# Attention scores: block-diagonal matmuls over the whole TensorE, or one head per matmul on strips of 32 rows

## The chip, the cores and the metric

The program runs on one core of one Trainium2 chip. What counts is the device time of one execution in microseconds. All engines start together; the time is that of the last instruction. The numbers on single instructions come from one profiled execution.

## What is computed

The reference is one transformer layer over 16 sequences of 128 tokens with 128 features. Cross attention with 16 heads of 8 dimensions each is followed by a mixture of experts with the two best of eight experts for each token.

```python
Q = _split_heads(q @ Wq.T)      # q is the layernorm of x
K = _split_heads(k @ Wk.T)      # k, v are the context
V = _split_heads(v @ Wv.T)
scores = jnp.einsum('bhqd,bhkd->bhqk', Q, K) / scale
scores = jnp.where(mask, NEG_INF, scores)
attn = jax.nn.softmax(scores, axis=-1)
out = jnp.einsum('bhqk,bhkd->bhqd', attn, V)
...
x = x + _L0_xattn_ref(_layernorm(x, axis=-1), ctx_1024, ctx_1024, mask_BxS2_if1, ...)
x = x + _L0_ffn_ref(_layernorm(x, axis=-1), L0_ffn_wg, L0_ffn_w1, L0_ffn_w3, L0_ffn_w2)
```

The scores of one head are a product over 8 features only. The kernel keeps float32 accuracy by splitting each value into a high and a low part of the float32r type.

## The kernel before, in words

Each engine runs a list of instructions written out by hand, and semaphores join the lists. The attention takes the 16 sequences (batches, `b` or `n`) in four quartets `u` of `QB = 4`. A fifth turn of the outer loop, `u == NQ`, finishes the last quartet.

**Stacks.** `front(u)` projects a quartet: for each group `g` of four heads it makes a query stack and a key stack in `st[:, u % 2, is_k, g, :]` with matmuls of 512 columns (L528). A stack has four strips of 32 partitions (`R = 32`), one for each head `j` of the group. In a strip lie the 8 features three times (as high, low and high parts in matching order) and two rows (24 and 25) that carry the mask. Rows 26 to 31 are not used.

**Scores twice.** The kernel forms every score tile twice. The first time queries are on the partitions (bank `s1`, L693), and VectorE takes the maximum over the keys of each (L1411). The second time keys are on the partitions (bank `s2`, L679), and ScalarE takes the exponential (L923) into `prob`. Before that the maximum must be subtracted: `m_neg` is rounded, transposed on TensorE (`transpose_maxima`), copied to `mT` (L1334), spread by GpSimd to a block form `m_bd` (L1026, four operations of 128x512 for a quartet), and added by a matmul with `ones_b` (L676) into the same bank.

**Block diagonals.** One matmul with 128 rows does the four heads of a group at once. Its moving operand has 512 columns, in which head `j` is nonzero only in strip `j` and in its own 128 columns. These operands are the slots `bd_slot(k, n)`; ScalarE clears six of them once (`clear_diagonal`, L810), and SyncE's queue copies the strips of the stacks into them, four DMAs of 64 KB for each slot (`block_diagonal`, L427; two of the first slot's by GpSimd's queue, L1018). TensorE waits for them in `diagonal_in`.

**Order of the work.** In the turn `u`, step `b`, group `g`, TensorE does the scores with keys on the partitions of quartet `u - 1` (batch `b`), then those with queries on the partitions of quartet `u` (batch `b - 1`). So step 0 of a turn has the former alone, steps 1 to 3 have both, and step 4 the latter alone. Between them come `values(n)` (L652, 16 products of 32 output rows on four column strips, each product two instructions), two transposes of the heads (L545), one back (L551) and the output projection (L558). Turn 0 has only the products for the maxima, turn 4 only those for the exponentials, together with routing and the preparation of the expert weights. The last 100 us are the experts.

`s1` has a ring of two banks (four in turn 0), `s2` a ring of two. TensorE waits for `max_done` and `prob_ready` before it reuses them. DVE waits for `s1_full`, ScalarE for `s2_full`.

## Time and profile before

| what | value |
|---|---|
| device time, median of 3 runs | 288.39 us (286.16 to 289.48) |
| span of the profiled execution | 289.2 us |
| TensorE busy, matmul | 220.1 us (76%) |
| VectorE (DVE) busy | 214.5 us (74%) |
| ScalarE (ACT) busy | 131.9 us (46%) |
| GpSimd (POOL) busy | 109.8 us (38%) |
| mean granted TensorE clock | 0.877 |

The profiled execution has no time of its own besides its span. The span is 0.8 us above the median and within the three runs. Busy time is summed over the whole span; which engine sets the time differs from stretch to stretch. A matmul's recorded duration includes its passage through the array, so the rate at which matmuls follow each other is read from the distance between their starts.

### The profile page before, as it was taken

The page shows a single profiled execution, that of the slowest core. Times are in us where ns is not written, and L with a number is a line of the kernel's source. Part 1 is how long each engine was busy: PE and PEld are TensorE (multiplying, and loading weights), DVE is VectorE, ACT ScalarE, POOL GpSimd, SP SyncE. Part 2 cuts the span into 40 slices and gives each one's busy share as a digit, 9 for nine tenths or more (in the row PEclk, how much of TensorE's full clock was granted, in tenths as well). Part 3 has the DMA queues.
Part 4 walks back from the last instruction along what each step waited for, and adds up shares of the span by engine and source line. Part 5 has one row for each costly group of instructions (what it writes and reads, how often), then busy time and mean ns, then how long its engine had stood idle before and what let it go on. Part 6 is the DMA issues. An engine that isn't in the chain of part 4 may idle for free.

```text
span 289.2 us, 5289 instructions
## 1 busy us (share of the span) xinstructions
PE 220.1 (76%) x1445; PEld 161.4 (56%) x1445; DVE 214.5 (74%) x619; ACT 131.9 (46%) x291; POOL 109.8 (38%) x120
## 2 busy tenths in 40 slices
PE   0787779998989988887667674688787789997620
PEld 0663456666757665665336542477566668886410
DVE  4779966688759867895977786568895568775596
ACT  5777127554665448342145546243334435453300
POOL 4310350121403070105486556104556565555530
PEclk9996579999999999979756799589899999999855
DMA  6954411353033302331602110421342232211807
GB/s 216 318 233 118 131 35 28 92 125 86 9 98 96 94 0 67 87 100 47 207 9 67 46 39 29 99 47 30 77 79 76 82 84 73 80 52 26 236 5 217
DMA packets 38108, 26.33 MB, mean 91 GB/s; under 512 B 4748, under 2 KB 35726, under 8 KB 37696
## 3 DMA queue, kind: packets, MB, share of 16 engines
q1 hardware_dynamic: 34848, 19.76, 25.5%
q0 software_dynamic: 2656, 5.40, 6.1%
q10 hardware_dynamic: 576, 0.83, 0.9%
q8 instruction: 13, 0.21, 0.3%
q14 instruction: 15, 0.12, 0.2%
HBM read 12.32 MB, written 6.31 MB: 64 GB/s over the span
## 4 chain that ended last, share of the span: by engine, by line
PE 42%; DVE 30%; issue 10%; SPq 8%; DMA 4%; ACT 2%; POOL 1%; another core or an unknown queue 1%; DVEq 0%; ACTq 0%; POOLq 0%
SPq L427 8%; PE bank L528 8%; DVE m_neg L1411 6%; PE bank L759 4%; PE bank L760 3%; PE bank L733 3%; PE bank L652 3%; DMA bd<-st 3%; PE bank L746 3%; PE bank L736 3%; PE bank L693 2%; PE bank L676 2%; PE bank L734 2%; PE bank L679 2%; PE bank L534 2%
## 5 line engine op out<-in xcount | busy, mean ns | idle before, releaser
L1411 DVE TENSOR_REDUCE m_neg<-bank 128x4 f32<-128x512 f32 x64 | 43.5, 684 | 15.4 <-PE bank L693 15.0
L1048 POOL DMA_INDIRECT ys<-big x39 | 38.1, 976 | 40.0 <-DVE big L1447 19.2
L923 ACT ACTIVATE big<-bank 128x512 f32<-128x512 f32 x64 | 37.4, 597 | 20.9 <-PE bank L679 20.0
L797 ACT ACTIVATE st<-bank 128x128 fp32r<-128x128 f32 (+1 forms) x78 | 22.6, 330 | 31.6 <-PE bank L746 16.1
L1004 POOL DMA_INDIRECT xg<-rows,rows_i x24 | 24.6, 1027 | 31.8 <-DVE rows_i L1218 11.6
L693 PE MATMUL bank<-bd,st 128*128 128x512 f32 x64 | 31.1, 509 | 4.7 <-DMA bd<-st 3.8
L676 PE MATMUL bank<-m_bd,ones_b 128*128 128x512 f32 x64 | 31.3, 489 | 2.1 <-ACT big L923 1.9
L759 PE MATMUL bank<-bd,st 128*128 x78 | 24.3, 332 | 9.8 <-DVE big L1447 6.2
L1355 DVE SCALAR_TENSOR_TENSOR st<-st_hi,cst,bank 128x512 fp32r<-128x512 f32 x32 | 23.3, 747 | 11.3 <-ACT st_hi L797 9.0
L1026 POOL TENSOR_TENSOR m_bd<-mT,cst 128x512 fp32r<-128x512 f32 x16 | 17.3, 1110 | 30.1 <-DVE mT L1334 30.0
L679 PE MATMUL bank<-bd,st 128*128 128x512 f32 x64 | 27.1, 423 | 0.0
L961 ACT ACTIVATE big<-bank 128x256 f32<-128x256 f32 x39 | 15.1, 387 | 24.2 <-PE bank L736 18.7
L1474 DVE TENSOR_TENSOR big<-big,bank 128x256 f32<-128x256 f32 x39 | 16.3, 418 | 12.7 <-ACT big L961 7.6
L733 PE MATMUL bank<-bd,st 128*128 x39 | 19.8, 509 | 5.5 <-DVE st L1435 4.8
L759 PEld LDWEIGHTS bank<-bd,st 128*128 128x128 f32 x78 | 15.6, 199 | 14.0 <-issue 13.1
L693 PEld LDWEIGHTS bank<-bd,st 128*128 128x128 f32 x64 | 14.2, 224 | 13.5 <-issue 6.7
L760 PE MATMUL bank<-bd,st 128*128 x78 | 21.5, 296 | 0.0
L1440 DVE TENSOR_TENSOR st<-bank,st 128x256 fp32r<-128x256 f32 x39 | 16.5, 422 | 5.5 <-ACT st L797 3.4
L988 POOL TENSOR_SCALAR ve<-mv 128x4 f32<-128x4 f32 x8 | 1.8, 230 | 46.7 <-DVE mv L1077 46.7
L1447 DVE TENSOR_REDUCE big<-bank 128x128 f32<-128x256 f32 x39 | 16.4, 421 | 4.1 <-PE bank L760 2.6
L652 PE MATMUL bank<-big 128*32 128x128 f32 x512 | 19.0, 294 | 0.0
L676 PEld LDWEIGHTS bank<-m_bd,ones_b 128*128 128x128 f32 x64 | 13.4, 209 | 9.0 <-issue 4.7
(174 smaller groups left out, 514.0 us busy)
## 6 DMA issues: line engine op xcount, KB each, us to landing
bd<-st SPq DMA_DIRECT2D x126, 64.0 KB, 2.0
big<-xg SPq DMA_DIRECT2D x39, 64.5 KB
raw<-in_L_ffn_w SPq DMA_DIRECT2D x2, 1024.0 KB, 9.3
raw<-ys SPq DMA_DIRECT2D x6, 256.0 KB
x_all<-in_x SPq DMA_DIRECT2D x4, 256.0 KB, 4.5
rows<-in_mask_BxS_if POOLq DMA_DIRECT2D x4, 256.0 KB, 5.2
ctx_all<-in_L_ffn_w SPq DMA_DIRECT2D x1, 1024.0 KB
ctx_all<-in_ctx SPq DMA_DIRECT2D x3, 256.0 KB, 5.2
```

The lines of the kernel that those rows point to most:

```text
L652: last = nc.tensor.matmul(ob[n % 2][R * j:R * (j + 1), half * P:(half + 1) * P], va[(n // QB) % 2][:, ((n % QB) * 4 + half * 2 + i) * NJ + ...
L676: nc.tensor.matmul(s2[k % 2][:, :], ones_b[:, b, :], m_bd[:, NJ * g:NJ * (g + 1), :].rearrange("p h q -> p (h q)"), start=True, stop=False)
L679: nc.tensor.matmul(s2[k % 2][:, :], st[:, (u - 1) % 2, 1, g, b * S:(b + 1) * S], bd_slot(0, n)[:, g, :, :].rearrange("p j q -> p (j q)"), ...
L693: nc.tensor.matmul(s1[k % s1_ring(u)][:, :], st[:, u % 2, 0, g, (b - 1) * S:b * S], bd_slot(1, n)[:, g, :, :].rearrange("p j q -> p (j q)" ...
L733: nc.tensor.matmul(both, t_lo[n % 2], first_high[:, :, bass.ds(col[n], I)], start=True, stop=False)
L759: nc.tensor.matmul(o, g_hi[n % GR][:, c * P:(c + 1) * P], w, start=(c == 0), stop=False)
L760: last = nc.tensor.matmul(o, g_lo[n % GR][:, c * P:(c + 1) * P], w, start=False, stop=(c == 1))
L923: nc.scalar.activation(prob[n % 2][:, NJ * g:NJ * (g + 1), :].rearrange("p h q -> p (h q)"), s2[k % 2][:, :], ACT.Exp, scale=SCALE).then_i ...
L1004: pool.indirect_dma_start(xg, bass.IndirectOffsetOnAxis(rows_i[:, n, k:k + 1], 0), sent_rows(n // QB)[:, n % QB, k, :], None, bounds_check ...
L1048: pool.indirect_dma_start(ys, bass.IndirectOffsetOnAxis(xt[n % XR][:, D:RW].bitcast(I32), 0), y_sb[n % YR], None, bounds_check=PAIRS - 1, ...
L1355: nc.vector.scalar_tensor_tensor(st[:, u % 2, is_k, g, :], st_hi[:, n % SH, :].bitcast(F32), cst[:, (C_CK if is_k else C_CQ):(C_CK if is_k ...
L1411: nc.vector.tensor_reduce(m_neg[:, H * (b - 1) + NJ * g:H * (b - 1) + NJ * (g + 1)], s1[k % s1_ring(u)][:, :].rearrange("p (j q) -> p j q" ...
```

## The change

The block diagonals, `m_bd`, `ones_b` and `bd` go. A score tile of 128x128 is now one matmul of its own: `scores(keys, queries, g)` multiplies 32 rows of a key stack by 32 rows of a query stack, at `tile_position=(R * g, 0)`. Step `g` now takes strip `g` of all four stacks, that is the heads `4 i + g`, where `i` is the number of the stack. The products with keys on the partitions use strip `g`, those with queries on the partitions strip `(g + 2) % 4`, in alternation. Both semaphore waits of a step (for `prob_ready` and for `max_done`) stand ahead of both products.

The rounded maxima, high and low, now go into rows 26 and 27 of the query strips. The key stacks hold ones in these rows, so the product itself adds the maxima. For each quartet eight DMAs copy 16 rows of `mT` each into one row of `st`: six on SyncE's queue and two on GpSimd's. Clearing of `va[1]` moves from DVE to GpSimd. The order of heads in `va`, `prob` and the rows of `Wo` follows.

```diff
-    c[:, C_CK] = np.where((r >= 8) & (r < 16), -1.0, 0.0)
+    c[:, C_CK] = np.where((r >= 8) & (r < 16), -1.0, np.where((r == MAX) | (r == MAX + 1), 1.0, 0.0))
...
+    c[:, C_ONE + 1] = (r == MAX) | (r == MAX + 1)
...
+        def maxima_in(engine, u):
+
+            for j in range(NJ):
+                engine.wait_ge(max_in[j], 32 * (u + 1))
+
+        def place_maxima(engine, u, j):
+
+            for a in range(2):
+                engine.dma_start(st[R * j + MAX + a:R * j + MAX + a + 1, u % 2, 0, :, :].rearrange("p g (b q) -> p (g b) q", q=S).bitcast(F32),
+                                 mT[R * j + 16 * a:R * j + 16 * (a + 1), :]).then_inc(max_in[j], 16)
...
-            for u in range(NQ + 1):
-                if u == NQ:
-                    sp.wait_ge(work_full, slot["V", NQ - 1] + 1)
-                    sp.wait_ge(ck_ready, NQ)
-                    sp.dma_start(raw[2], w2).then_inc(in_w2, 16)
...
+            for u in range(NQ):
+                taken(sp, ("MT", u))
+                for j in range(NJ - 1):
+                    place_maxima(sp, u, j)
+            sp.wait_ge(work_full, slot["V", NQ - 1] + 1)
+            sp.wait_ge(ck_ready, NQ)
+            sp.dma_start(raw[2], w2).then_inc(in_w2, 16)
...
+            def keys_wait(n, g):
+
+                k = NG * n + g
+                if n % QB == 0:
+                    pe.wait_ge(max_in[g], 32 * (n // QB + 1))
+                if k >= 2:
+                    pe.wait_ge(prob_ready, k - 1)
+
+            def queries_wait(n, g):
+
+                k, u = NG * n + g, n // QB
+                if n % QB == 0 and g == 0:
+                    stacks_in(pe, u, 0)
+                    stacks_in(pe, u, 1)
+                if k >= s1_ring(u):
+                    pe.wait_ge(max_done, k - s1_ring(u) + 1)
+
+            def scores(keys, queries, g):
+
+                if keys is not None:
+                    keys_wait(keys, g)
+                if queries is not None:
+                    queries_wait(queries, g)
+                for i in range(NG):
+                    if keys is not None:
+                        u, b = divmod(keys, QB)
+                        rows, tokens = slice(R * g, R * (g + 1)), slice(b * S, (b + 1) * S)
+                        by_key = nc.tensor.matmul(s2[g % 2][:, i * P:(i + 1) * P], st[rows, u % 2, 1, i, tokens], st[rows, u % 2, 0, i, tokens],
+                                                  start=True, stop=True, tile_position=(R * g, 0))
+                    if queries is not None:
+                        v, c = divmod(queries, QB)
+                        own, mine = query_rows(g), slice(c * S, (c + 1) * S)
+                        part = slice(R * own, R * (own + 1))
+                        by_query = nc.tensor.matmul(s1[(NG * queries + g) % s1_ring(v)][:, i * P:(i + 1) * P], st[part, v % 2, 0, i, mine],
+                                                    st[part, v % 2, 1, i, mine], start=True, stop=True, tile_position=(R * own, 0))
+                if keys is not None:
+                    by_key.then_inc(s2_full, 1)
+                if queries is not None:
+                    by_query.then_inc(s1_full, 1)
...
-                            nc.tensor.matmul(s2[k % 2][:, :], ones_b[:, b, :],
-                                             m_bd[:, NJ * g:NJ * (g + 1), :].rearrange("p h q -> p (h q)"),
-                                             start=True, stop=False)
-                            nc.tensor.matmul(s2[k % 2][:, :], st[:, (u - 1) % 2, 1, g, b * S:(b + 1) * S],
-                                             bd_slot(0, n)[:, g, :, :].rearrange("p j q -> p (j q)"),
-                                             start=False, stop=True).then_inc(s2_full, 1)
...
-                            nc.tensor.matmul(s1[k % s1_ring(u)][:, :], st[:, u % 2, 0, g, (b - 1) * S:b * S],
-                                             bd_slot(1, n)[:, g, :, :].rearrange("p j q -> p (j q)"),
-                                             start=True, stop=True).then_inc(s1_full, 1)
...
+                        scores(QB * (u - 1) + b if u >= 1 and b < QB else None, QB * u + b - 1 if u < NQ and b >= 1 else None, g)
...
-            clear_diagonal(0)
-            clear_diagonal(1)
+            act.wait_ge(in_c, 16)
...
-            for j in range(2, NJ):
-                rows = slice(R * j, R * (j + 1))
-                pool.dma_start(bd_slot(1, 0)[rows, :, j, :].bitcast(F32), st[rows, 0, 1, :, 0:S].bitcast(F32)).then_inc(first_half, 16)
+            own(nc.gpsimd.memset(va[1][:, :, :], 0.0))
...
                 if u:
-
                     taken(pool, ("MT", u - 1))
-                    if u >= 2:
-                        pool.wait_ge(s2_full, NG * QB * (u - 1))
-                    for g in range(NG):
-                        nc.gpsimd.tensor_tensor(m_bd[:, NJ * g:NJ * (g + 1), :], mT[:, :].unsqueeze(1).to_broadcast([P, NJ, P]),
-                                                cst[:, C_HEAD + NJ * g:C_HEAD + NJ * (g + 1)].unsqueeze(2).to_broadcast([P, NJ, P]),
-                                                ALU.mult).then_inc(mbd_ready, 1)
+                    place_maxima(pool, u - 1, NJ - 1)
```

TensorE before, in turn 1 around the values of the second batch. L676 and L679 are the scores by key, L693 the scores by query, L652 the values, L551 and L558 the transpose back and the projection:

```order
L676 MATMUL bank3<-m_bd,ones_b 128x512
L679 MATMUL bank3<-bd,st 128x512
L693 MATMUL bank1<-bd,st 128x512
L652 MATMUL bank5<-big 32x128 x16
L551 MATMUL bank4<-cst,on 128x128
L676 MATMUL bank2<-m_bd,ones_b 128x512
L679 MATMUL bank2<-bd,st 128x512
L693 MATMUL bank0<-bd,st 128x512
L558 MATMUL bank4<-wo_s,onT 128x128
```

TensorE after, in turn 1 around the values of the first batch. L659 is the score by key, L665 by query, L627 the values:

```order
L659 MATMUL bank3<-st 128x128
L665 MATMUL bank1<-st 128x128
L659 MATMUL bank3<-st 128x128
L665 MATMUL bank1<-st 128x128
L627 MATMUL bank4<-big 32x128 x16
L659 MATMUL bank2<-st 128x128
L665 MATMUL bank0<-st 128x128
L659 MATMUL bank2<-st 128x128
L665 MATMUL bank0<-st 128x128
```

Three matmuls of 512 columns have become eight of 128, in alternation between two strips; the places of the values, transposes and projections in the row stay.

SyncE's queue before, from the last loads of the input to the table that the experts need:

```order
L404 DMA ctx_all<-in_ctx 128x512
L414 DMA raw<-in_L_ffn_w 128x2048 x2
L427 DMA bd<-st 32x4x128 x122
L434 DMA ctx_all<-in_L_ffn_w 128x2048
L427 DMA bd<-st 32x4x128 x4
L460 TENSOR_LOAD tab
```

SyncE's queue after, the same piece:

```order
L400 DMA ctx_all<-in_ctx 128x512
L410 DMA raw<-in_L_ffn_w 128x2048 x2
L378 DMA st<-mT 1x16x128 x24
L418 DMA ctx_all<-in_L_ffn_w 128x2048
L434 TENSOR_LOAD tab
```

The load of the third expert weight now stands behind the maxima of the last quartet.

## Rows read from the trace of the kernel before

**Rows 1.** Page, the chain that ended last: share of the span by engine.

```profile
PE 42%; DVE 30%; issue 10%; SPq 8%; DMA 4%; ACT 2%; POOL 1%; another core or an unknown queue 1%; DVEq 0%; ACTq 0%; POOLq 0%
```

**Rows 2.** Windows: stretch, its length, busy time of each engine, clock, DMA share, GB/s.

```profile
25.59:38.77 13.18, 10.40 (x24) 5.69 (x25) 12.62 (x32) 3.08 (x5) 3.12 (x4) 0.57 0.43 115
...
51.66:69.47 17.81, 17.22 (x187) 11.79 (x188) 14.99 (x39) 9.73 (x21) 3.13 (x4) 1.00 0.44 105
...
113.86:145.12 31.26, 24.15 (x215) 17.24 (x216) 25.14 (x81) 9.98 (x23) 8.29 (x9) 0.85 0.39 108
145.12:188.48 43.36, 29.43 (x214) 19.18 (x215) 30.48 (x109) 20.87 (x44) 24.39 (x25) 0.74 0.18 50
```

**Rows 3.** Timeline of TensorE in turn 2: start, duration, line.

```profile
82.98 0.40 PE L693 MATMUL bank<-bd,st 128*128 128x512 f32 x1
83.31 1.08 PE L652 MATMUL bank<-big 128*32 128x128 f32 x32
84.32 0.50 PE L676 MATMUL bank<-m_bd,ones_b 128*128 128x512 f32 x1
84.66 0.39 PE L679 MATMUL bank<-bd,st 128*128 128x512 f32 x1
84.89 0.39 PE L693 MATMUL bank<-bd,st 128*128 128x512 f32 x1
85.12 0.40 PE L676 MATMUL bank<-m_bd,ones_b 128*128 128x512 f32 x1
```

**Rows 4.** Timelines of TensorE: narrower matmuls.

```profile
7.84 2.05 PE L600 MATMUL bank<-wvT,ctx_all 128*128 128x128 f32 x8 [7.84 <-DMA wvT<-in_L_xattn_Wv]
...
69.47 1.06 PE L600 MATMUL bank<-wvT,ctx_all 128*128 128x128 f32 x8
...
117.22 0.95 PE L572 MATMUL bank<-wgT,cT 128*128 128x8 f32 x8
...
239.43 0.28 PE L760 MATMUL bank<-bd,st 128*128 x1
239.55 0.28 PE L759 MATMUL bank<-bd,st 128*128 x1
```

**Rows 5.** Timeline of TensorE's weight loads, at the values of Rows 3.

```profile
83.31 0.81 PEld L652 LDWEIGHTS bank<-big 128*32 128x32 f32 x32 [0.37 <-issue]
```

**Rows 6.** Timeline of all engines where turn 0's scores begin.

```profile
18.78 3.57 DVE L1355 SCALAR_TENSOR_TENSOR st<-st_hi,cst,bank 128x512 fp32r<-128x512 f32 x5 [0.18 <-PE bank L528]
...
22.72 1.76 DVE L1123 MEMSET big<- 128x2048 f32 x1 [0.38 <-issue]
...
23.25 1.95 PE L693 MATMUL bank<-bd,st 128*128 128x512 f32 x4 [2.48 <-DMA bd<-st]
...
24.77 0.67 DVE L1411 TENSOR_REDUCE m_neg<-bank 128x4 f32<-128x512 f32 x1
```

**Rows 7.** Timeline of TensorE: first score by query of turn 3.

```profile
113.86 0.47 PE L693 MATMUL bank<-bd,st 128*128 128x512 f32 x1 [0.28 <-DMA bd<-st]
```

**Rows 8.** Page, costliest groups: busy us, mean ns, idle before and releaser.

```profile
L1411 DVE TENSOR_REDUCE m_neg<-bank 128x4 f32<-128x512 f32 x64 | 43.5, 684 | 15.4 <-PE bank L693 15.0
...
L923 ACT ACTIVATE big<-bank 128x512 f32<-128x512 f32 x64 | 37.4, 597 | 20.9 <-PE bank L679 20.0
```

**Rows 9.** The line of the block diagonals' DMAs: ns of issue, us to landing.

```profile
L427 SPq DMA_DIRECT2D bd<-st x126: 585/601/1538, 19.7 to 157.8; - x126
...
DMA to landing us min/median/max: 2.0/2.0/4.7
```

**Rows 10.** Timeline of all engines at the beginning of turn 4.

```profile
145.63 0.29 DVE L1334 COPY mT<-bank 128x128 f32<-128x128 f32 x1
...
147.43 0.76 PE L676 MATMUL bank<-m_bd,ones_b 128*128 128x512 f32 x1 [0.18 <-POOL m_bd L1026]
...
150.84 1.29 DVE L1314 TENSOR_TENSOR bd<-raw,bd 128x512 fp32r<-128x512 f32 x2
...
153.56 1.12 PE L534 MATMUL bank<-cst,st_hi 128*128 128x128 f32 x4 [2.96 <-DVE st_hi L1098]
```

157 lines of the change are left out of this document (41 added, 116 removed).

## The prediction

> **What bounds the kernel now.** I read the chain of work that ended last, then the windows, stage by stage, and then the timelines of single steps. The chain gives TensorE 42%, DVE 30%, and 12% to SyncE's queue and DMAs [rows 1]: three candidates, and the change touches all of them. The windows tell them apart [rows 2]. In turn 0 (25.59 to 38.77) DVE is busy 12.62 of 13.18 us, and TensorE's clock is mostly at its lower level: DVE bounds it. In steps 1 to 4 of turn 1 (51.66 to 69.47) TensorE is busy 17.22 of 17.81 us, DVE 14.99: TensorE bounds it, but DVE stands 2.8 us behind. Turn 2 repeats turn 1. In turns 3 and 4 (31.26 and 43.36 us) neither is above about 80%: there, chains from engine to engine set the pace. SyncE's queue is on the chain only because its DMAs run one behind the other, 0.60 us each to issue [rows 9]; what counts is where TensorE waits for them: 2.48 us once at the start [rows 6] and some 0.3 us at the first score by query of each of turns 1 to 3, of which turn 3's is shown [rows 7]. So the block diagonals' traffic and ScalarE's clearing weigh little, and the question is what TensorE's instructions cost.
>
> **The pair of scores on TensorE.** Before, a step has three matmuls of 512 columns, whose starts lie 0.23 us apart (84.66, 84.89, 85.12), so 0.70 us [rows 3]. After, it has eight of 128 columns, each with its own weights of 128 columns. No row shows a matmul on a strip of rows, nor a float32r matmul of 128 columns, so I bound both. A full-array matmul of only 8 columns costs at most 0.95/8 = 0.12 us, and one of 256 columns of float32r (the experts' L759, L760; `bd` is by then the expert weights) 0.12 us too [rows 4]: below 256 columns the load of 128 weight columns sets the rate. I estimate 0.112 for one. If the two strips in alternation work side by side, a step costs four of these, 0.45 us; if they take turns, eight, 0.90. For side by side speak the values: 32 instructions on four column strips take 1.08 us [rows 3] and their loads 0.81 [rows 5], a quarter of what 32 would take one after another. Those are column strips with narrow loads, so this is near, not the same. I take 0.45. One step saves 0.25 us, and the twelve steps with both products in a turn save 3.0.
>
> **What strips cost elsewhere.** The array must change between its whole, column strips and row strips. Into the values: the last L693 starts at 82.98 and would be through at 83.21; the values start at 83.31, 0.10 late. Out of them: eight waves of 0.11 from 83.31 end at 84.19; the next starts at 84.32, and its successor 0.34 later where 0.23 is usual, since its load was not hidden: 0.24 together [rows 3]. Before, a batch has two such changes. After, seven: the transposes L545, L551 and the projection L558 now also stand between row strips. Five more for each of four batches are 20 in a turn. Their load was partly exposed already, so I take the 0.10 for each, 2.0 us in a turn; at 0.24 it is 4.8. The Trainium skill ("TensorEngine Tiling (Array Packing)", Key Properties) says that changing the tiling mode drains TensorE. The gap at the values agrees with that; by it the changes cannot be free, and it speaks against this change. It also says that different tiles can load and multiply in parallel, which no trace here shows for strips of rows.
>
> The four steps 4 of turns 0 to 3 have only queries: 0.45 instead of 0.23 each group. DVE takes 684 ns for each maximum [rows 8] and hides that; without it, 0.9 us a turn. Turn 0 is the same at the lower clock: L600 there takes 2.05 us for eight instructions against 1.06 [rows 4], so a group costs up to 4 x 0.26 = 1.0, or less with the next strip beside it, against 13.18/16 = 0.82 of DVE: about even, up to 3 us if it is not.
>
> Both semaphore waits now stand ahead of the pair, so a score by key also waits for DVE's maximum two groups back; queued behind it are ScalarE's exponential and the values. In turns 1 and 2 DVE becomes the next bound: 14.99 of 17.81. That caps the gain at 2.8 a turn. **Turns 1 and 2: 2 x (-3.0 + 2.0) = -2.0 us**, between 2 x -2.8 and 2 x +1.8. **Turn 3**, where DVE and TensorE are both at some 80% [rows 2], half of that for one turn: **-0.5**, between -1.5 and +0.9.
>
> **The waits that go.** At the start the last stack is ready at 18.78 + 3.57 = 22.35, and the first matmul starts at 23.25; DVE meanwhile clears `va[1]` (22.72, 1.76 us) and takes its first maximum at 24.77 [rows 6]. After, both DMA and clearing are gone from here; four matmuls from 22.4 at up to 0.26 each let DVE start at about 23.3: **-1.5 us**, and all of it counts, since DVE bounds the turn. The memset on GpSimd lies in the idle time while TensorE makes the first stacks. The three waits of rows 7: **-0.9** (0 to -1.2); the wait for an exponential of the `s2` ring [rows 8] comes up behind them. ScalarE's six clearings, DVE's `ones_b` and GpSimd's `m_bd` run beside longer work: nothing.
>
> **The maxima by DMA.** From `mT` on, SyncE issues six DMAs of 0.60 us; each lands 2.0 us later [rows 9]. The first pair is in at +3.2 us, the third at +5.6; GpSimd's pair at about +3.4. In turns 1 to 3, the stacks of the next quartet (28 matmuls of 512 columns, 6.4 us at the distance of rows 3) stand between and hide it, if narrowly; were it not hidden, it would cost up to 5.6 a turn. In turn 4 nothing stands between: `mT` is ready at 145.92, so the first score comes at 149.1 instead of 147.43 and the third at 151.5 [rows 10]. Behind it are an exponential (0.6), two weight copies on ScalarE and then DVE's L1314, which began at 150.84 right behind other work; it begins about 0.5 us later. The fourth group waits for L534 at 153.56 anyway. **+0.5**, between 0 and +1.7. SyncE's load of the third weight moves behind the maxima, to about 149.5; its first user is tick 12 of 20 in a turn of 43 us. GpSimd loses four m_bd operations and gains two DMAs, so the row sends behind them come no later.
>
> **Turn 4 otherwise.** Sixteen groups of 0.45 instead of 0.47: nothing. Fifteen to twenty more changes of the array's form, some 0.10 each, half on the chain: **+0.9**, up to +3.
>
> **Sum:** -1.5 - 0.9 - 2.0 - 0.5 + 0.5 + 0.9 = -3.5 us. The span was 289.2 and becomes 285.7; set against the median of 288.4, that gives **284.9 us**. The experts' 100 us are untouched.
>
> **The rivals.**
> *A. Everything is hidden.* Changes of form cost nothing more, and DVE bounds turns 1 and 2: -5.6 there, -1.5 in turn 3, -1.5 - 1.2 at the waits, 0 in turn 4: -9.8, **278.6 us**. For it: DVE's 2.8 us; against it: the gaps in rows 3.
> *B. Changes of form cost 0.24 each.* +3.6 in turns 1 and 2, +0.9 in turn 3, +2.5 in turn 4, less 2.4: +4.6, **293 us**. Slower from about 0.16 for a change on.
> *C. Strips of rows take turns.* The change then doesn't do what its title says. A pair costs 0.90, 5.4 us more a turn than forecast, in turn 3 half: 13.5 above the forecast, **298 us**. Slower once a pair costs over some 0.57. Against it: rows 5.
> *D. A float32r matmul of 128 columns runs like plain float32.* L600, plain float32, needs two instructions for a product, up to 0.13 us each at the full clock, 0.26 at the lower [rows 4]. All float32r matmuls of before have 256 or 512 columns, so nothing in the trace excludes it. A pair then costs 0.7 to 1.0, turn 0 at the low clock up to 1.3 to 2 a group against 0.82: +8 there or more, +3.5 for turns 1 and 2 with the changes, +4 in turn 4, less 2.4: **about 301 us**.
>
> **How the numbers follow.** Forecast 0.42 (its own range 281 to 288), A 0.15, B 0.15, C 0.11, D 0.17. Three executions lay 3.3 us apart, so about 1% (2.9 us) is what a measurement can tell from no change. The forecast is faster by over 1% in three quarters of its range and A always: 0.47. Within 1%: a quarter of the forecast and a part of B and C: 0.19. Slower: 0.34. The range of 278 to 299 takes in A, the forecast, B and half of C and D.
>
> **What the profile after would show.** Starts of L659 about 0.11 apart with an L665 between, a pair of groups at 0.45 (right), 0.90 (C); two records for each product would be D. The first maximum near 23.3. Windows of steps 1 to 4 in turns 1 and 2 at about 16.8, DVE over 88% busy. The distance from the last L659 or L665 to a transpose and back prices a change of form. The first score of turn 4 about 3.4 us after `mT`. I would be wrong if DMAs into a single row took much longer than 2.0 us, or if DVE, waited for earlier now, held back the exponentials.

## The result, and the profile after

The changed kernel takes **318.28 us** (median of 4 runs, 317.71 to 321.57), the kernel before in the same runs 288.94 (286.16 to 291.12). The ratio is 1.109, with a 95% interval of 1.100 to 1.118. The prediction was 284.9, range 278 to 299: wrong in size and in sign. The span of the profiled execution is 315.9 us, 26.7 above the 289.2 of before. Executions of one kernel differ by their clock (e6 below: 300.5 us at a mean clock of 0.783, 316.9 at 0.718), so a median is of all of them, a ratio only of those within 1.5% of the fastest, and no ratio stands where the spread is wide.

The page of the kernel after, its busy time, its granted clock in 40 slices of the span (tenths, 9 is full), and the chain that ended last:

```profile
PE 251.4 (80%) x1765; PEld 204.6 (65%) x1765; DVE 213.4 (68%) x615; ACT 123.4 (39%) x285; POOL 96.3 (30%) x113
...
PEclk9996579555695555955555555555999999999755
...
PE 59%; DVE 21%; DMA 7%; issue 6%; ACT 4%; POOL 2%; SPq 0%; POOLq 0%; ACTq 0%; DVEq 0%
```

The same clock row of the kernel before:

```profile
PEclk9996579999999999979756799589899999999855
```

TensorE's share of the chain grows from 42% [rows 1] to 59%, and DVE's falls from 30% to 21%. The clock rows show why. Before, the clock is at its upper level (2.4 GHz) from turn 1's stacks through turn 2 and turn 3's stacks. After, it is at 5 tenths, the lower level (1.2 GHz), for most of turns 1 to 4. The mean granted clock is 0.709 against 0.877.

By stretch, the windows of the kernel after: turn 0; turns 1 and 2, each from its own last stack to the first stack of the next; turns 3 and 4; the experts. Columns as in rows 2; the clock is the third number from the right.

```profile
25.59:40.60 15.01, 12.31 (x73) 11.22 (x67) 13.44 (x33) 1.77 (x4) 3.10 (x4) 0.53 0.08 19
48.60:81.80 33.20, 30.25 (x287) 24.39 (x287) 19.00 (x48) 12.83 (x27) 3.10 (x4) 0.58 0.03 9
90.20:123.90 33.70, 30.35 (x287) 24.31 (x287) 19.95 (x56) 12.82 (x27) 2.54 (x3) 0.57 0.00 1
131.80:172.10 40.30, 35.60 (x307) 28.79 (x306) 28.43 (x90) 13.38 (x29) 9.35 (x10) 0.55 0.05 15
172.10:215.60 43.50, 34.52 (x237) 26.48 (x236) 27.07 (x102) 20.50 (x43) 18.82 (x21) 0.50 0.22 68
215.60:315.90 100.30, 71.25 (x445) 61.46 (x445) 73.95 (x232) 37.24 (x117) 46.82 (x48) 0.87 0.31 83
```

The same cuts of the kernel before (its turns 3 and 4 in one row):

```profile
47.70:70.60 22.90, 21.34 (x208) 14.22 (x206) 17.95 (x47) 13.01 (x28) 3.13 (x4) 1.00 0.42 101
78.30:102.30 24.00, 21.47 (x208) 14.30 (x206) 18.98 (x55) 13.64 (x29) 2.57 (x3) 1.00 0.35 88
109.90:185.00 75.10, 53.67 (x431) 35.43 (x429) 56.61 (x190) 33.45 (x72) 32.08 (x34) 0.81 0.26 71
185.00:289.10 104.10, 76.33 (x445) 63.83 (x445) 75.15 (x232) 36.61 (x118) 47.13 (x48) 0.88 0.33 85
```

Turn 1 loses 33.2 - 22.9 = 10.3 us, turn 2 loses 9.7, turns 3 and 4 together 83.8 - 75.1 = 8.7. The first stack matmul of turn 1 comes at 40.6 instead of 38.9, 1.7 late; the experts take 3.8 less, for which no cause was looked for. With +0.2 for the three blocks of stacks between, that is the 26.7. TensorE is above 90% busy in turns 1 and 2 and DVE at 57 to 59%: TensorE bounds them alone.

What happens inside turn 1, in finer windows of the kernel after:

```profile
48.60:51.40 2.80, 1.87 (x17) 1.53 (x16) 1.93 (x4) 2.48 (x6) 0.00 (x0) 1.00 0.00 0
51.40:53.70 2.30, 2.27 (x52) 2.00 (x52) 1.54 (x4) 1.56 (x3) 0.00 (x0) 1.00 0.00 0
53.70:60.00 6.30, 5.81 (x67) 4.61 (x67) 4.42 (x14) 2.56 (x5) 1.86 (x3) 0.50 0.01 4
...
81.80:84.40 2.60, 2.60 (x9) 1.94 (x8) 0.96 (x3) 1.34 (x3) 1.00 (x2) 0.50 0.03 7
84.40:90.20 5.80, 5.79 (x26) 4.29 (x24) 4.16 (x7) 4.09 (x7) 0.00 (x0) 1.00 0.05 11
```

The clock is still 1.00 in step 0 and the first pairs of step 1. At 53.7 it falls to 0.50, though TensorE is 92% busy from then on; it comes back at 84.4, in the stacks of turn 2, whose matmuls take 128 rows and 512 columns. The fall repeats in turns 2 and 3, just before 95 and 136; turn 4 has no stacks, and the clock stays at 0.50 from 136 to the end of turn 4. Being busy is plainly not what the clock goes by alone.

TensorE on both sides of that fall, in its timeline of the kernel after (L659 by key, L665 by query, L627 the values):

```profile
51.43 0.32 PE L659 MATMUL bank<-st 32*128 32x128 f32 x1 [0.20 <-ACT big L892]
51.44 0.32 PE L665 MATMUL bank<-st 32*128 32x128 f32 x1
51.60 0.27 PE L659 MATMUL bank<-st 32*128 32x128 f32 x1
51.60 0.27 PE L665 MATMUL bank<-st 32*128 32x128 f32 x1
...
51.92 0.32 PE L659 MATMUL bank<-st 32*128 32x128 f32 x1
...
52.31 0.27 PE L659 MATMUL bank<-st 32*128 32x128 f32 x1
...
52.51 1.08 PE L627 MATMUL bank<-big 128*32 128x128 f32 x32
...
57.34 0.41 PE L659 MATMUL bank<-st 32*128 32x128 f32 x1
...
57.55 0.41 PE L659 MATMUL bank<-st 32*128 32x128 f32 x1
...
58.10 1.93 PE L627 MATMUL bank<-big 128*32 128x128 f32 x32
```

The strips do what the title says. L659 and L665 start within 0.01 us of each other, and a pair of groups takes 51.92 - 51.43 = 0.49 us. From the last of a pair to the values are 0.20 us (52.31 to 52.51), where 0.11 is usual between products: the change of form costs 0.09. After the fall the same products stand 0.21 apart (57.34, 57.55) instead of 0.11, and the values take 1.93 us instead of 1.08.

### The profile page after: what moved, and what is told of

It reads as the page before. It is cut to its first block, busy times and chain, and to the rows that moved or that the text cites. A ratio compares the mean times of both kernels' runs of the same rounds, so it can differ in the third digit from the quotient of the medians.

```text
span 315.9 us, 5743 instructions
## 1 busy us (share of the span) xinstructions
PE 251.4 (80%) x1765; PEld 204.6 (65%) x1765; DVE 213.4 (68%) x615; ACT 123.4 (39%) x285; POOL 96.3 (30%) x113
## 4 chain that ended last, share of the span: by engine, by line
PE 59%; DVE 21%; DMA 7%; issue 6%; ACT 4%; POOL 2%; SPq 0%; POOLq 0%; ACTq 0%; DVEq 0%
PE bank L659 12%; PE bank L502 9%; PE bank L627 7%; DVE m_neg L1360 4%; PE bank L665 4%; PE bank L532 3%; PE bank L519 3%; PE bank L508 3%; PE bank L742 2%; PE bank L716 2%; DMA ys<-big 2%; PE bank L719 2%; PE bank L717 2%; PE bank L525 2%; PE bank L743 2%
## 5 line engine op out<-in xcount | busy, mean ns | idle before, releaser
L659 PE MATMUL bank<-st 32*128 32x128 f32 x256 | 51.5, 386 | 5.7 <-ACT big L892 2.9
L659 PEld LDWEIGHTS bank<-st 32*128 32x128 f32 x256 | 43.2, 282 | 16.2 <-issue 8.2
L665 PE MATMUL bank<-st 32*128 32x128 f32 x256 | 51.6, 404 | 2.6 <-DVE st L1305 1.9
L665 PEld LDWEIGHTS bank<-st 32*128 32x128 f32 x256 | 44.3, 298 | 5.7 <-issue 4.7
L1305 DVE SCALAR_TENSOR_TENSOR st<-st_hi,cst,bank 128x512 fp32r<-128x512 f32 x32 | 23.1, 748 | 12.1 <-ACT st_hi L864 12.1
L742 PE MATMUL bank<-weights,st 128*128 x78 | 23.0, 316 | 8.9 <-DVE big L1395 8.9
L627 PE MATMUL bank<-big 128*32 128x128 f32 x512 | 29.6, 407 | 0.0
L864 ACT ACTIVATE st_hi<-bank,cst 128x512 fp32r<-128x512 f32 x32 | 22.0, 688 | 12.9 <-PE bank L502 12.7
L716 PE MATMUL bank<-weights,st 128*128 x39 | 19.6, 501 | 7.1 <-DVE st L1383 7.0
L928 ACT ACTIVATE big<-bank 128x256 f32<-128x256 f32 x39 | 15.0, 384 | 22.9 <-PE bank L719 22.9
L627 PEld LDWEIGHTS bank<-big 128*32 128x32 f32 x512 | 21.2, 161 | 3.4 <-issue 0.3
L742 PEld LDWEIGHTS bank<-weights,st 128*128 128x128 f32 x78 | 14.9, 190 | 11.1 <-issue 9.8
L378 POOL DMA_DIRECT2D st<-mT x8 | 4.2, 529 | 58.1 <-DVE mT L1287 58.1
L743 PE MATMUL bank<-weights,st 128*128 x78 | 20.8, 286 | 0.0
## 6 DMA issues: line engine op xcount, KB each, us to landing
big<-xg SPq DMA_DIRECT2D x39, 64.5 KB, 1.9
```

The source lines that it names most:

```text
L627: last = nc.tensor.matmul(ob[n % 2][R * g:R * (g + 1), half * P:(half + 1) * P], va[(n // QB) % 2][:, (n % QB) * H + h, :], prob[n % 2][:, ...
L659: by_key = nc.tensor.matmul(s2[g % 2][:, i * P:(i + 1) * P], st[rows, u % 2, 1, i, tokens], st[rows, u % 2, 0, i, tokens], start=True, sto ...
L665: by_query = nc.tensor.matmul(s1[(NG * queries + g) % s1_ring(v)][:, i * P:(i + 1) * P], st[part, v % 2, 0, i, mine], st[part, v % 2, 1, i ...
L716: nc.tensor.matmul(both, t_lo[n % 2], first_high[:, :, bass.ds(col[n], I)], start=True, stop=False)
L742: nc.tensor.matmul(o, g_hi[n % GR][:, c * P:(c + 1) * P], w, start=(c == 0), stop=False)
L743: last = nc.tensor.matmul(o, g_lo[n % GR][:, c * P:(c + 1) * P], w, start=False, stop=(c == 1))
```

## The experiments

Fifteen more kernels ran. "Turn 1" is the same stretch as above, from the turn's last stack matmul to the next turn's first, with its granted clock.

| kernel | device time, median (lowest to highest), us | ratio to before, 95% | turn 1: us at clock | turn 2: us at clock |
|---|---|---|---|---|
| before | 288.94 (286.16 to 291.12) | 1 | 22.9 at 1.00 | 24.0 at 1.00 |
| after | 318.28 (317.71 to 321.57) | 1.109 (1.100 to 1.118) | 33.2 at 0.58 | 33.7 at 0.57 |
| e1_warm | 368.56 (357.57 to 375.70) | 1.244 (1.232 to 1.256) | 43.9 at 0.57 | 44.8 at 0.55 |
| e2_split | 302.41 (300.05 to 303.22) | 1.043 (1.036 to 1.051) | 27.3 at 1.00 | 28.3 at 1.00 |
| e3_wide | 357.57 (353.32 to 365.98) | 1.227 (1.217 to 1.237) | 35.4 at 0.82 | 45.6 at 0.57 |
| e4_dve_clear | 317.84 (313.72 to 322.82) | - | 29.2 at 0.71 | 34.7 at 0.54 |
| e5_full_rows | 306.37 (303.05 to 311.88) | - | 24.6 at 1.00 | 31.9 at 0.79 |
| e6_rows64 | 313.36 (300.50 to 316.87) | - | 31.6 at 0.63 | 35.1 at 0.54 |
| e7_q_strips | 302.78 (300.85 to 308.98) | 1.050 (1.041 to 1.059) | 28.0 at 1.00 | 29.1 at 1.00 |
| e8_k_strips | 338.46 (338.26 to 338.94) | 1.176 (1.169 to 1.183) | 40.0 at 0.57 | 41.3 at 0.59 |
| e9_k_strips_plus | 359.57 (347.44 to 363.29) | - | 45.5 at 0.59 | 46.8 at 0.60 |
| e10_q_strips_less | 329.16 (328.01 to 331.64) | 1.146 (1.139 to 1.153) | 36.4 at 0.62 | 39.5 at 0.56 |
| e11_max_rows | 308.47 (304.87 to 310.59) | 1.066 (1.060 to 1.073) | 30.8 at 0.78 | 31.4 at 0.89 |
| e12_k_strips_next | 330.47 (329.70 to 343.94) | 1.136 (1.126 to 1.145) | 41.5 at 0.63 | 33.3 at 0.90 |
| e13_max_rows_plus | 309.34 (308.42 to 310.86) | 1.065 (1.057 to 1.073) | 31.9 at 0.89 | 31.8 at 0.89 |
| e14_max_pool | 302.59 (301.34 to 309.78) | 1.050 (1.044 to 1.057) | 24.2 at 0.86 | 25.1 at 1.00 |
| e15_max_pool_plus | 304.76 (303.19 to 306.24) | 1.057 (1.051 to 1.064) | 24.4 at 1.00 | 25.0 at 1.00 |

The times of a turn come from one profiled execution of each kernel. It is the longest or nearly the longest of its kernel for e1 (375.7 us), e6 (316.5), e9 (363.3) and e11 (310.6), and the shortest or nearly so for e4 (313.7) and e5 (303.3); so the turns of different kernels compare only roughly.

### Does the fall of the clock depend on the rows that a product fills?

**e1_warm**: the changed kernel with one matmul of 128 rows and 512 columns ahead of every step's products.

```diff
+                if keys is not None or queries is not None:
+                    spot = s2[g % 2] if keys is not None else s1[(NG * queries + g) % s1_ring(queries // QB)]
+                    nc.tensor.matmul(spot[:, :], ws_hi[:, 0, 0, :], ws_hi[:, 0, :, :].rearrange("p g c -> p (g c)"), start=True, stop=True)
                 for i in range(NG):
```

> The changed kernel plus one matmul for each step, ahead of its products: all 128 rows, 512 columns, into the bank that the products then overwrite; its result is never used. 92 of them add 0.23 us each at the full clock, 21 us of work, and bring two more changes of the array's form a step. Theory 1 (the changed kernel is slow because TensorE's clock stands at its lower level through turns 1 to 4, and it does so because the scores now come as narrow matmuls on strips of rows): the clock in turns 1 and 2 comes back to 0.9 or more, and although work is added the time falls, to some 295 to 305 us. Theory 2 (the strips are slow by themselves, by changes of form and by the two waits ahead of a pair; the clock only follows an array that idles): the added work comes on top, 330 us or more.

Measured: 368.56 us. Turn 1 has TensorE busy for all of its 43.9 us, and the clock is at 0.57. One full product a step does not hold it up; this cure fails. The windows on both sides of the fall in turn 1:

```profile
60.30:69.50 9.20, 9.20 (x54) 6.72 (x52) 5.22 (x9) 6.76 (x11) 0.00 (x0) 1.00 0.00 1
69.80:107.60 37.80, 37.80 (x269) 28.11 (x269) 16.49 (x42) 9.61 (x20) 3.11 (x4) 0.50 0.03 8
```

TensorE has not paused once in the 9 us before the clock falls. So a wait just ahead is not needed for the fall; it came here without one.

**e2_split**: the kernel before, each of the products L679 and L693 cut in four of 128 columns; all keep 128 rows.

```diff
-                            nc.tensor.matmul(s1[k % s1_ring(u)][:, :], st[:, u % 2, 0, g, (b - 1) * S:b * S],
-                                             bd_slot(1, n)[:, g, :, :].rearrange("p j q -> p (j q)"), ...
+                            for j in range(NJ):
+                                last = nc.tensor.matmul(s1[k % s1_ring(u)][:, j * P:(j + 1) * P], st[:, u % 2, 0, g, (b - 1) * S:b * S],
+                                                        bd_slot(1, n)[:, g, j, :], start=True, stop=True)
```

> The kernel before with its L679 and L693 cut into four matmuls of 128 columns each, all 128 rows as before: 128 rows, narrow. Each takes 0.112 us instead of a quarter of 0.23, so a pair costs 0.23 + 8 x 0.112 = 1.13 us instead of 0.70. If the narrow matmuls, in which the load of the weights sets the rate, are what lets the clock fall, the clock in turns 1 and 2 falls to about 0.5 as in the changed kernel, and the time goes over 325 us. If it is the 32 rows, the clock stays at 1.0 in turns 1 and 2 and the time is that of the added 0.43 us a pair: 5 us in each of turns 1 and 2, some 3 in turn 3, a little in turns 0 and 4: 300 to 306 us.

Measured: 302.41 us, clock 1.00 in both turns. Narrow products alone cost 4.4 us in turn 1 (27.3 less 22.9) and leave the clock up.

**e3_wide**: the changed kernel, each product on its 32 rows but with 512 columns. The scores are then no longer the reference's, since each product runs over all four batches.

```diff
-                        by_key = nc.tensor.matmul(s2[g % 2][:, i * P:(i + 1) * P], st[rows, u % 2, 1, i, tokens], st[rows, u % 2, 0, i, tokens],
+                        by_key = nc.tensor.matmul(s2[g % 2][:, :], st[rows, u % 2, 1, i, tokens], st[rows, u % 2, 0, i, :],
```

> The changed kernel with each product on a strip 512 columns wide instead of 128: it multiplies a batch's keys by the queries of all four batches, over the whole bank, and so leaves out the right scores. 32 rows, wide. If 32 rows are what lets the clock fall, it stays at about 0.5 in turns 1 to 4, and a pair costs 4 x 0.43 = 1.7 us: 350 us or more. If narrow matmuls are, the clock stays at 1.0, a pair costs 4 x 0.23 = 0.92 and the time is 300 to 310 us, less than the changed kernel's 318 with four times the columns.

Measured: 357.57 us. The clock falls with wide products of 32 rows too. Turn 1 and turn 2 are the same program apart from a few small operations, 35.4 us at 0.82 and 45.6 at 0.57: a first price of the clock.

**e5_full_rows** and **e6_rows64**: the changed kernel with the same 128 columns, the same order and the same DMAs, on all 128 rows (e5), or on two strips of 64 (e6). Each product then sums over four or two heads, so the scores are not the reference's. Two more things change with it. The first group of a turn waits for all the maxima at once, and e5 has no changes of form between its products and the transposes and projections.

```diff
-                        by_key = nc.tensor.matmul(s2[g % 2][:, i * P:(i + 1) * P], st[rows, u % 2, 1, i, tokens], st[rows, u % 2, 0, i, tokens],
-                                                  start=True, stop=True, tile_position=(R * g, 0))
+                        by_key = nc.tensor.matmul(s2[g % 2][:, i * P:(i + 1) * P], st[:, u % 2, 1, i, tokens], st[:, u % 2, 0, i, tokens],
+                                                  start=True, stop=True)
```

> The changed kernel with every product of 128x128 on all 128 rows instead of 32: it adds up the scores of four heads, so the right scores are left out, and the same number of matmuls, the DMAs of the maxima and the joined waits remain. They can no longer run side by side: a pair costs 8 x 0.112 = 0.90 us at the full clock instead of 0.45. Theory 1 (32 rows let the clock fall, and the low clock is what costs): the clock in turns 1 and 2 stays at 1.0 and the time is 293 to 300 us, 20 below the changed kernel, though TensorE's products take twice as long side by side with nothing. Theory 2 (the structure of the change costs: number of matmuls, joined waits, maxima by DMA, changes of form): the time stays above 310 us.

> The changed kernel with 64 rows for each product, on two strips of 64: scores of two heads are added, the right ones left out. The two products of a pair stand on different halves in every step and can run side by side, 0.45 us a pair, with the same changes of form as in the changed kernel. It asks where between 32 and 128 rows the clock turns. If it stays at 1.0 in turns 1 and 2, the time is what I had forecast for the change itself, 283 to 290 us; if it falls as with 32 rows, 315 to 322.

Measured: e5 takes 306.37 us, 12 below the changed kernel, although its products no longer run side by side. In its timeline of TensorE they stand 0.11 us apart, a pair of groups 0.90, as the forecast had it for products in turn:

```profile
51.15 0.28 PE L665 MATMUL bank<-st 128*128 128x128 f32 x1
51.26 0.27 PE L659 MATMUL bank<-st 128*128 128x128 f32 x1
51.37 0.28 PE L665 MATMUL bank<-st 128*128 128x128 f32 x1
```

Its turn 1 keeps the clock and takes 24.6 us. The same order with 32 rows takes 33.2. So with half the speed for the scores the turn is 8.6 us shorter. The changes of form that e5 saves, put at 2.0 us a turn in the prediction, are less than the 5.4 us (12 x 0.45) that its products cost more; the clock makes the difference.

In turn 2 e5 loses a part of it, so 293 to 300 was too low:

```profile
84.00:97.40 13.40, 13.40 (x110) 12.29 (x109) 6.16 (x17) 3.86 (x7) 1.78 (x3) 0.50 0.01 2
97.80:112.40 14.60, 12.95 (x157) 11.83 (x155) 11.59 (x34) 7.01 (x16) 0.36 (x1) 1.00 0.00 1
```

The clock can fall without any strip, then, but it comes back inside the turn, while in the changed kernel it stays down until the next stacks. e6's executions run from 300.5 to 316.9 us, from below e5's fastest (303.1) to almost the changed kernel's; where between 32 and 128 rows the clock turns, it does not tell.

### What does a lower clock cost?

**e4_dve_clear**: the changed kernel, `va[1]` cleared on DVE behind turn 0's stacks, as before.

```diff
-            own(nc.gpsimd.memset(va[1][:, :, :], 0.0))
...
+                if u == 0:
+                    clear_values(1)
```

> The changed kernel with the clearing of va[1] put back from GpSimd to DVE, at the beginning of turn 0. In the changed kernel one of DVE's four normalisations waits for 2 us beside GpSimd's memset, and everything behind it starts 2 us later. If the memset is the cause, the first stack matmul starts 2.0 us earlier; DVE then spends 1.8 us on the clearing ahead of its first maximum, which partly stands beside TensorE's first products: a gain of 0 to 1.5 us, 317 to 318.5. If the pause has another cause, the stack starts as late as in the changed kernel and the time rises to 320.

Two things come out. First, the clearing on GpSimd was not free. The start of the kernel after, all engines:

```profile
8.20 4.07 DVE L1062 TENSOR_SCALAR rows<-x_all,mv,rstd 128x128 f32<-128x128 f32 x4 [0.47 <-POOL rstd L956]
...
10.06 1.81 POOL L981 MEMSET big<- 128x2048 f32 x1
...
14.01 0.77 PE L502 MATMUL bank<-ck_hi,ws_hi 128*128 128x512 f32 x1 [0.56 <-DVE ck_lo L1102]
```

and of e4:

```profile
8.21 2.07 DVE L1057 TENSOR_SCALAR rows<-x_all,mv,rstd 128x128 f32<-128x128 f32 x4 [0.48 <-POOL rstd L956]
...
12.01 0.76 PE L502 MATMUL bank<-ck_hi,ws_hi 128*128 128x512 f32 x1 [0.56 <-DVE ck_lo L1100]
```

With GpSimd's memset beside it DVE's four normalisations take 2.0 us longer, and TensorE's first stack comes 2.0 us later. Second, e4 has the program of the changed kernel from turn 1 on, yet its turn 1 takes 29.2 us at a clock of 0.71 instead of 33.2 at 0.58. In e4 the clock falls only at 60, two batches into the turn instead of one. So one stretch of the changed program can be seen at the upper level: from the values of the first batch to those of the second, in e4 and in the kernel before:

```profile
51.37:55.50 4.13, 3.49 (x69) 2.87 (x67) 3.72 (x13) 2.66 (x6) 0.45 (x2) 1.00 0.02 6
52.75:57.22 4.47, 4.47 (x48) 3.00 (x47) 3.55 (x13) 2.61 (x6) 0.51 (x2) 1.00 0.39 101
```

TensorE has 0.98 us less to do there, and the stretch is 0.34 us shorter: TensorE now waits, 0.64 us of it for a maximum of DVE, which is busy for 3.72 of 4.13 us. Four such stretches make a turn, for which the forecast was -1.0. The next one is 0.43 us longer than before (55.50 to 60.69 against 57.22 to 61.98), with its last 0.7 us at the lower clock, so one stretch does not stand for the turn.

The whole turn at full clock was not measured. An estimate: with 2 x (1 - 0.58) x 33.2 = 27.9 us at the lower level in turn 1 of the changed kernel and 16.9 in e4's, the 11.0 us between them cost 4.0, and without any the turn would take 23.1. If the 27.9 us all ran at half speed, it would be 19.3. My working for the turn, 22.9 - 1.0 = 21.9, lies between. The total is not clearly moved (317.84; 313.72 and 314.23 in two runs, 321.44 and 322.82 in two with a clock of 0.69).

### Which part of the change lets the clock fall?

**e7_q_strips**: the kernel before, only the scores by query on strips. **e8_k_strips**: the changed kernel, the scores by query back on block diagonals as one product of 512 columns; the clearing on DVE.

```diff
 e7
-                            nc.tensor.matmul(s1[k % s1_ring(u)][:, :], st[:, u % 2, 0, g, (b - 1) * S:b * S], ...
+                            for i in range(NG):
+                                last = nc.tensor.matmul(s1[k % s1_ring(u)][:, i * P:(i + 1) * P], st[part, u % 2, 0, i, mine],
+                                                        st[part, u % 2, 1, i, mine], start=True, stop=True, tile_position=(R * g, 0))
 e8
-                        by_query = nc.tensor.matmul(s1[...][:, i * P:(i + 1) * P], st[part, v % 2, 0, i, mine], ...
+                    nc.tensor.matmul(s1[(NG * queries + g) % s1_ring(v)][:, :], st[:, v % 2, 0, g, c * S:(c + 1) * S],
+                                     bd_slot(queries)[:, g, :, :].rearrange("p j q -> p (j q)"), start=True, stop=True).then_inc(s1_full, 1)
```

> One half of the change alone: the kernel before, with only the scores by query (L693) on strips of 32 rows; the scores by key stay as block diagonals with ones_b. A step is 2 x 0.23 us on the whole array, 4 x 0.11 on a strip and two changes of form at 0.2: 1.3 us at the full clock. Theory 1: the narrow strips again let the clock fall in turns 1 and 2, though over a third of the array's time is wide matmuls of 128 rows (the added fillers did not hold it either): 335 to 350 us. If wide matmuls in this share hold the clock: 305 to 315.

> The other half alone: the changed kernel with the scores by query back on block diagonals (16 slots of DMAs a kernel, three slots cleared, va[1] cleared by DVE), the scores by key on strips with the maxima in the spare rows. A step is 4 x 0.11 us on a strip, 0.23 on the whole array and two changes of form: 1.0 us at the full clock, against 0.70 before and 0.9 in the changed kernel at the low clock. Theory 1: low clock again, a step at 1.6 us or more: 330 to 345 us. If the clock holds: 300 to 308.

Measured: e7 302.78 us with a clock of 1.00 in turns 1 and 2, not the fall that theory 1 had, and a little below the 305 to 315 of the other case; e8 338.46 with 0.57 and 0.59. Strips of 32 rows do not bring the clock down by being there. A step of e7 has two full products and four on a strip, one of e8 one full product and four on a strip. The next three runs ask whether that is the difference.

**e10_q_strips_less**: e7 without L676, the matmul that adds the maxima.

```diff
-                            nc.tensor.matmul(s2[k % 2][:, :], ones_b[:, b, :],
-                                             m_bd[:, NJ * g:NJ * (g + 1), :].rearrange("p h q -> p (h q)"),
-                                             start=True, stop=False)
```

> The kernel e7 (before, with the scores by query as four matmuls of 32 rows) without the matmul that adds the maxima; it leaves that subtraction out, so its exponentials are not the reference's. A step now has one full product and four on a strip, as e8. By the count of work it should gain up to 16 x 0.23 = 3.7 us a turn: 290 to 298 us against e7's 302.8. Theory 1 (the share of full products decides the clock): the clock falls in turns 1 and 2 as in e8, their distance between stacks grows from 28 and 29 us to 35 to 42, and the whole takes 320 to 340 us, slower for less work. Rival (something else of e8 holds its clock down): the clock stays at 1.0 in turns 1 and 2 and the whole takes 290 to 300 us.

Measured: **329.16 us, 26 more for 64 matmuls less**. Turn 1 goes from 28.0 us at a clock of 1.00 to 36.4 at 0.62. In e7:

```profile
48.80:76.80 28.00, 26.89 (x255) 18.90 (x253) 18.53 (x47) 13.26 (x28) 3.11 (x4) 1.00 0.19 48
```

and in e10:

```profile
47.10:83.50 36.40, 35.28 (x239) 26.02 (x238) 19.16 (x48) 13.11 (x27) 3.10 (x4) 0.62 0.14 37
...
49.80:55.90 6.10, 6.09 (x58) 4.29 (x58) 3.62 (x11) 3.48 (x7) 0.00 (x0) 1.00 0.21 52
```

Here too TensorE is busy without a pause for the 6 us before the clock falls, at 56.

**e9_k_strips_plus** and **e12_k_strips_next**: the opposite, e8 with full products added. In e9 one stands ahead of the four strips in each of the 64 groups that have keys. In e12 it stands behind them, next to the other full product, and only where a group has both: 36 of them, 12 instead of 16 in each of turns 1 to 3 and none in turn 4.

```diff
 e9
+                if keys is not None:
+                    nc.tensor.matmul(s2[g % 2][:, :], ws_hi[:, 0, 0, :], ws_hi[:, 0, :, :].rearrange("p g c -> p (g c)"), start=True, stop=True)
                 for i in range(NG):
 e12
+                    if keys is not None:
+                        nc.tensor.matmul(s1[(NG * queries + g) % s1_ring(v)][:, :], ws_hi[:, 0, 0, :], ...
                     nc.tensor.matmul(s1[(NG * queries + g) % s1_ring(v)][:, :], st[:, v % 2, 0, g, c * S:(c + 1) * S],
```

> The kernel e8 (scores by query as one matmul of 512 columns on block diagonals, scores by key as four matmuls of 32 rows) with one more matmul of 512 columns and 128 rows ahead of each group's four products by key; its result is overwritten, so the output is e8's. At full clock these 64 matmuls cost 64 x 0.23 = 14.7 us. Theory 1, the granted clock depends on how much of TensorE's time goes to matmuls on the full array: the mixture of a step is now that of e7 (two full products and four on a strip), so the clock stays at 1.0 in turns 1 and 2, their distance between stacks falls from some 40 us to 28 to 30, and the whole takes 300 to 315 us, 20 us or more below e8's 338 although it does more. Rival, something else of e8 holds the clock down (the products by key on strips, the pairing under two waits, the DMAs into single rows): the clock stays low and the 64 matmuls are added at the lower rate, 345 to 365 us.

> The kernel e9, with the extra matmul of 512 columns and 128 rows directly ahead of the full score by query, so that the two full products of a step stand next to each other behind the four on a strip, as in e7. Its result is overwritten. Theory 2, the order decides (short pieces of full work between strips do not hold the clock, longer ones do): the clock stays at 1.0 in turns 1 and 2, the distances between stacks fall to 28 to 31 us, the whole takes 300 to 318 us. Rival, the clock falls for another reason of e8 (TensorE's waits in step 0 of a turn, and strips by key that carry the maxima): as e9, 347 to 363 us with a clock of 0.70 to 0.75.

Measured: e9 359.57 us, clock 0.59 and 0.60; the mixture of e7 is not enough, and the rival has it. e12 330.47 us, 29 less in the median and 18 between the shortest executions (347.4 and 329.7). It is not e9 in another order alone, as its expectation has it: it has 28 full products fewer, which at 0.23 us each (0.43 at the lower clock) are 6 to 12 us. Its turns are split; the windows of e12:

```profile
46.70:88.20 41.50, 39.09 (x251) 27.55 (x251) 18.48 (x47) 13.27 (x28) 3.10 (x4) 0.63 0.12 33
96.00:129.30 33.30, 29.16 (x251) 20.92 (x251) 19.56 (x55) 13.84 (x29) 2.55 (x3) 0.90 0.13 33
```

In steps 1 to 3 the two kernels have the same instructions in another order, so the order may play a part; but the missing products of step 0 changed with it, and the two were not separated. e12 did not hold the clock in turn 1, nor bring the time to the 300 to 318 expected. Two turns of nearly the same program have different clocks here: 41.5 us at 0.63, 33.3 at 0.90.

### The other half of the change alone

**e11_max_rows**: the kernel before with all its block diagonals; only the maxima go by DMA, straight into rows 26 and 27 of the query block diagonals, and L676, `m_bd` and `ones_b` go. It is the part of the change that takes work from TensorE without any strip.

```diff
-                            nc.tensor.matmul(s2[k % 2][:, :], ones_b[:, b, :], m_bd[...], start=True, stop=False)
...
+            for j in strips:
+                for a in range(2):
+                    row, at = R * j + MAX + a, R * j + 16 * a
+                    if b == 0:
+                        engine.dma_start(bd[row:row + 1, 3:6, :].rearrange("p k (g j q) -> p (k g) j q", g=NG, j=NJ)[:, :, j, :].bitcast(F32),
+                                         mT[at:at + 12, :]).then_inc(max_in[j // 2 * 2], 16)
+                    else:
+                        engine.dma_start(bd_slot(0, n)[row:row + 1, :, j, :].bitcast(F32), mT[at + 12:at + 16, :]).then_inc(max_in[1], 16)
```

> The other half of the change alone: before, with all products on block diagonals of 128 rows, but the maxima go by DMA into rows 26 and 27 of the query block diagonals (16 DMAs for a quartet, 12 on SyncE's queue and 4 on GpSimd's), and the matmul that adds them, its operand on GpSimd and the block of ones go. A step has two products of 512 columns in place of three. At full clock this takes 16 x 0.23 = 3.7 us out of TensorE in a turn, of which at most 2.8 count in turns 1 and 2 before DVE bounds them, half in turn 3; turn 4's first score comes up to 1.7 us later and DVE has some eight small operations more for each quartet. Theory 1 with the clock unharmed: -2.8 x 2 - 1.4 + 1 + 1 = -5, 283 us, between 279 and 287. Rival, the thinner mixture of full products lets the clock fall in turns 1 and 2: 292 to 305 us.

**e13_max_rows_plus**: e11 with a full product in the place of L676, its result overwritten.

```diff
+                            nc.tensor.matmul(s2[k % 2][:, :], ws_hi[:, 0, 0, :], ws_hi[:, 0, :, :].rearrange("p g c -> p (g c)"), start=True, stop=True)
                             nc.tensor.matmul(s2[k % 2][:, :], st[:, (u - 1) % 2, 1, g, b * S:(b + 1) * S],
```

> The kernel e11 with one extra matmul of 512 columns and 128 rows ahead of each score by key, in the place of the matmul that added the maxima before; its result is overwritten, so it is pure extra work, 64 x 0.23 = 14.7 us of it at full clock. Theory 3 (the clock falls in e11 because TensorE is less busy while it waits for ScalarE and DMAs, and the removed matmul kept it busy): the clock stays at 1.0 in turns 1 and 2, the distances between stacks fall from 30.8 and 31.4 us to 23 to 27, and the whole takes 288 to 299 us, faster than e11 although it does more. Rival (the fall in e11 comes from the wait of 1.0 us for the key block diagonals alone, or from the DMAs): the clock falls as in e11, and the extra matmuls come on top, 310 to 325 us.

Measured: 308.47 and 309.34 us. Neither expectation for e11 holds in full, because my version has a wait of its own, which the line of the score by key in e11 shows (groups of the window 49 to 80; busy, mean, idle and its releasers):

```profile
L699 PE MATMUL bank<-bd,st 128*128 128x512 f32 x16 | 9.0, 573 | 5.6 <-DMA bd<-mT 4.5 <-ACT big L939 1.1
```

The fourth batch's maxima stand too late in SyncE's queue. In e13 the same wait is 5.5 us in one piece (59.0 to 64.5), and only in its last microsecond does the clock fall; windows of e13's turn 1:

```profile
46.30:60.00 13.70, 11.52 (x102) 7.27 (x100) 9.52 (x25) 8.48 (x17) 3.14 (x4) 1.00 0.29 74
60.00:63.00 3.00, 0.00 (x0) 0.00 (x0) 0.00 (x0) 0.00 (x0) 0.00 (x0) 1.00 0.32 91
63.00:66.00 3.00, 1.47 (x4) 1.10 (x5) 0.00 (x0) 0.24 (x1) 0.00 (x0) 0.64 0.21 51
66.00:69.00 3.00, 3.00 (x30) 2.17 (x32) 2.35 (x6) 0.96 (x2) 0.00 (x0) 0.50 0.25 62
```

The clock is then low for some 7 us, though TensorE is 100% busy from 65 on, and comes back within turn 1. In the changed kernel, with all scores on strips, it stays low until the next stacks.

**e14_max_pool** and **e15_max_pool_plus**: e11 and e13 with the fourth batch's eight DMAs on GpSimd's queue.

```diff
-                        place_maxima(sp, QB * (u - 1) + b, range(NJ))
...
+                    if u < NQ:
+                        place_maxima(pool, QB * (u - 1) + 3, range(NJ))
```

> The kernel e11 with the eight DMAs of the fourth batch's maxima on GpSimd's queue in place of SyncE's, so that they no longer stand behind 7 us of other issues. Theory A (e11's clock fell because of its waits alone): the clock stays near 1.0 in turns 1 and 2, the distance between stacks goes to 20.5 to 22.5 us in turn 1 against 22.9 before, with two full products a step and DVE as the bound, and the whole takes 278 to 286 us. Theory B (the product that adds the maxima kept the clock up): the wait is gone but the clock falls in part of turns 1 and 2, mean 0.75 to 0.9 there, distances of 25 to 29 us, and the whole takes 291 to 303 us.

> The kernel e14 with one full product of 512 columns in the place of the one removed, its result overwritten: 64 x 0.23 = 14.7 us of extra work at full clock. Theory A: it keeps the clock as e14 does and costs what it did before, 285 to 291 us, 3 to 8 above e14. Theory B: the clock is 1.0 in turns 1 and 2 only here, and it takes 285 to 292 us, below e14 although it does more.

Measured: 302.59 and 304.76 us; both times missed. The windows of turns 1 and 2 and of 3 and 4 together, in e14:

```profile
48.80:73.00 24.20, 20.93 (x192) 13.14 (x190) 18.45 (x53) 13.51 (x29) 7.13 (x12) 0.86 0.34 85
80.70:105.80 25.10, 18.68 (x192) 11.53 (x190) 19.55 (x61) 13.52 (x29) 6.53 (x11) 1.00 0.28 72
113.60:199.30 85.70, 52.11 (x398) 33.35 (x396) 55.52 (x196) 33.17 (x72) 39.87 (x52) 0.68 0.21 60
```

and of turn 2 in e15:

```profile
79.40:104.40 25.00, 21.52 (x208) 14.37 (x206) 19.56 (x61) 13.73 (x29) 6.53 (x11) 1.00 0.29 74
```

In turn 2 both have the clock at 1.00, and 16 products less (18.68 us busy instead of 21.52) give nothing: 25.1 against 25.0. The time comes back as waits of TensorE for the block diagonals, one of 1.97 us in step 3 of e14. So theory A is right on the clock in turn 2 and wrong on the gain. In turn 1 e14's clock is 0.86 and e15's 1.00, which is theory B, but both take some 24.3 us, and each clock is of one execution. The loss of both kernels lies in turns 3 and 4, 85.7 us (e14) against 75.1 before; TensorE waits 3.3 us there for the first DMAs of the maxima, and the mean clock is 0.68. No version here beats the kernel before.

## Why the prediction was wrong

**The step that failed is one that was not there.** All durations in the sum were taken at the full clock, and the table of rivals had none in which the granted clock of turns 1 to 4 changes. The row was in view: before, the clock is 1.00 in steps 1 to 4 [rows 2], and I took this for a property of the place, not of the work that stands there. The clock was even named in the prediction, for turn 0 only. Its price in turn 1 is 10 to 14 us by the two estimates at e4 (33.2 less 23.1 to 19.3), and turn 2 loses about as much. For turns 3 and 4 before had 0.81 and after 0.55 and 0.50; how much of the 8.7 that is was not separated.

Step by step:

- **The pair of scores, 0.45 us side by side**: 0.49 at full clock. Right in mechanism, 0.04 short. Rivals C (strips take turns) and D (128 columns of float32r at the rate of float32) are refuted: the two start within 0.01 us, and e5's 128-column products stand 0.11 apart.
- **Changes of form at 0.10**: 0.09 into the values. At the upper clock in e4 the last product before two transposes starts at 54.30 and they at 54.54, 0.13 more than the usual 0.11; behind them the next product comes at 54.91, some 0.15 late if each transpose takes 0.11. So 0.10 was low, and 2.0 us a turn nearer to 3.
- **Turns 1 and 2, -2.0**: measured +20.0. At full clock the one stretch seen whole, in e4, is 0.34 us shorter; for a whole turn the two estimates give -3.6 to +0.2, so its sign is open. That TensorE bounds them was only half right: in e4 DVE takes back 0.64 of the 0.98 us, and 2.8 us less gave nothing in e14's turn 2.
- **Turn 3, -0.5, and turn 4, +0.5 and +0.9**: together measured +8.7, at the low clock; not to be separated here.
- **Start, -1.5**: measured +1.7 to the first stack of turn 1. "The memset on GpSimd lies in the idle time" was wrong: it lay beside DVE's normalisation and cost 2.0. The other part came true in small: with the clearing back on DVE (e4), the first maximum starts at 24.34 instead of 24.77 [rows 6], not at 23.3, since the clearing stands there again. In the changed kernel it starts at 25.82: 1.05 late, of the 2.0 that the memset costs. That DVE bounds turn 0 was right: it is busy for 13.44 of 15.01 us.
- **Three waits for block diagonals, -0.9**: they are gone; the gain is smaller than the clock's loss and cannot be read apart.
- **Maxima by DMA, first score at +3.2 us behind `mT` in turn 4, hidden in turns 1 to 3**: +2.5 (`mT` is written at 172.27 + 0.29 = 172.56, the score starts at 175.04). The group of L659 has 1.3 us of waits for these DMAs in all, and turn 4's two, 1.16 and 0.16, make them up: in the other turns they are hidden. Right in mechanism, 0.7 too long. The kernel after, at the start of turn 4:

```profile
172.27 0.29 DVE L1287 COPY mT<-bank 128x128 f32<-128x128 f32 x1
...
172.59 3.66 SPq L378 DMA_DIRECT2D st<-mT  x6
...
175.04 1.11 PE L659 MATMUL bank<-st 32*128 32x128 f32 x4 [1.16 <-DMA st<-mT]
```

**What is shown and what is not.** Shown for turns 1 and 2, 20 of the 27 us of span: the low clock takes the loss (e5 against after; e4, e3 and e12 at two clocks). Shown too: the width of the products does not bring it (e2 against e3), thinner work on the array does (the changed kernel against e5, and e10 against e7 by 26 us, in all executions), and waits just ahead are not needed (e1, e10). Pointed to by one execution each: a product of 128 rows keeps the clock up even where its result is thrown away (turn 1 of e15 against e14). With full products alone the clock fell too, in e5's turn 2, e13 and e14, but came back within the turn. Open: the rule. The number of rows, the mixture of full products and strips (e7 and e9 have the same in a step) and the time busy (e1 is at 100%) each fail alone; what the order does, e9 and e12 leave open.

## What to carry to other kernels

Before a change that makes TensorE's products smaller, thinner or fewer, read the granted clock of the stretch and make "it falls to 1.2 GHz" a rival of its own, priced by the same work at either level: here values took 1.08 or 1.93 us. Removing a matmul from a stretch at full clock is no safe gain: ask what keeps the clock there, and which transfer is late next. And an operation moved to GpSimd may stretch what DVE does beside it. Not every one does: in the kernel before, a multiplication on GpSimd of 1.27 us, from 8.18, ran beside the same normalisations, which took 2.08. Look at both in the timeline.

## What was not expected of the hardware

- Two strips of 32 rows start together (0.00 to 0.01 us apart) and load and multiply side by side, 0.49 us for 8 products of 128 columns. The Trainium skill ("TensorEngine Tiling (Array Packing)", Key Properties) has it that different tiles can do this; the trace agrees.
- The clock fell beneath products of 32 rows in 92% and even 100% busy stretches (0.50 in 53.7 to 60.0; 0.57 in e1), and came back within each block of full stacks of turns 1 to 3 (2.6 us into turn 2's, at 84.4).
- 64 matmuls fewer made a kernel 26 us slower (e7 to e10), and 64 more cost 0.9 us in one (e11 to e13) and 2.2 in another (e14 to e15), where their own time, at 0.23 each, is 14.7.
- A memset of 128x2048 on GpSimd of 1.81 us stretched DVE's four normalisations of 128x128 beside it from 2.07 to 4.07 us.
